# Mixture-of-experts stage: other row chunks, high parts by plain conversion, and the first expert's order of splitting

## The chip, the core and the metric

One core of one Trainium2 chip. The metric is the device time of one execution of the whole kernel in microseconds (us). The kernel before has a median of 5408.9 us in 3 runs (5398.77 to 5411.32). The engines: PE (TensorE, matrix products; its weight loads are listed as PEld and run beside the products), DVE (VectorE), ACT (ScalarE), POOL (GpSimd), and SP, which here only starts transfers.

## The reference, cut to what matters

Two transformer layers work on 16 batches of 512 tokens with 256 features. The change is in the last step only, a mixture of 8 experts in which each token goes to its best two experts:

```python
C = int(round(K * T * CAP_RATIO / E))          # K=2, T=8192, CAP_RATIO=1.05, E=8: 2150 slots an expert
buf = jnp.zeros((E, C + 1, D), xf.dtype).at[e_ord, pos].add(x_disp)[:, :C]
h = jax.nn.gelu(jnp.einsum('ecd,edh->ech', buf, W1) + b1[:, None, :], approximate=False)
y = jnp.einsum('ech,ehd->ecd', h, W2) + b2[:, None, :]
out = jnp.einsum('tk,tkd->td', cw, y_tk)       # cw: the gate's weights, y_tk: y of a token's two slots
```

D is 256 and the hidden width H is 1024. 2150 slots are 17 row tiles of 128 (`SLOT_TILES = 17`).

## The kernel before, in words

Eight stages run one after the other with a barrier between them (`STAGES`). The last, `experts` (L2384), takes the final 841 us of the trace. The earlier stages have filled a buffer in memory (`xbuf`) with each expert's rows. For expert n the 17 row tiles are worked in chunks of `QT = 4` tiles: `CHUNKS` (L2387) gives 4, 4, 4, 4 and 1 tiles, so `NC = 5`.

All products are made in float32r, a type that keeps fewer bits of a float32. To keep the accuracy each operand is split in a high and a low part, both float32r, and the product is high*high + high*low + low*high. The high part is got in two instructions: a mask (`bitwise_and` with `HIGH_BITS`) writes a cut copy, a conversion writes the cut copy as float32r. The low part is the operand minus the cut copy. This is done for the weights (`split_weights`, 8 pieces of 128x512 an expert: 0 to 3 are W1, 4 to 7 are W2), for the turned rows (`read_turned`, straight from PSUM) and for the hidden layer (`split_hidden`).

PE's order in an expert, for each chunk c: `hidden` for k = 0 to 7 (six matmuls each, L2653 to L2655; the moving operand has as many columns as the chunk has rows, 512 or 128), then `turn` of the *next* chunk (transposes, L2644, two for each tile), then `rows` for each tile i (16 matmuls, L2665 with 512 columns and L2667 with 256, into one of two PSUM banks). Before an expert PE waits for all 8 pieces of its weights, before a chunk's `hidden` for both `t_read` of its rows, in `rows` of tile 0 for each high and low part, and in `rows` of every tile for the bank of two tiles ago to be read (`y_read`).

ACT, for each k: the Gelu (L2562) of the PSUM bank, and after it the conversion of the cut copy of k-1 (`high_hidden`, L2552). The conversion of k = 7 follows at the chunk's end. Gelu k waits until the low part of k-4 is made.

DVE, in program order for each chunk: for k = 0 to 7 the mask (L2601) and the subtraction (L2604) of `split_hidden`; `read_turned` of the next chunk (two masks L2588, then L2592 and L2593 twice); then for each tile `read_rows` (L2611, L2613), and between tiles of chunks 1, 2 and 3 the pieces of the next expert's weights (`PIECES_IN`). Ahead of the first expert it splits all 8 pieces of weights and then reads the first turned rows.

POOL, for each tile: a multiplication by the gate's weight (L2523) and an indirect transfer that adds the rows to the output (L2527). SP loads rows and weights one or two chunks ahead. `expert_passes` (L2448) writes experts 0, 1, 6 and 7 straight out and runs experts 2 to 5 in a loop of two passes.

Of the kernel before, what the change touches and what calls it, by code (L numbers as in the profile page):

```python
# [8 lines left out]
ALU = mybir.AluOpType  # L9
AX = mybir.AxisListType.X  # L10
F32 = mybir.dt.float32
# [3 lines left out]
U32 = mybir.dt.uint32  # L15

P = 128
# [2366 lines left out]
def experts(nc, d):  # L2384


    CHUNKS = [(a, min(a + QT, SLOT_TILES)) for a in range(0, SLOT_TILES, QT)]  # L2387
    NC = len(CHUNKS)
    HC = HID // P
    NY = SLOT_TILES  # L2390
    RING = 4
# [4 lines left out]
    with ExitStack() as ctx:  # L2396
# [6 lines left out]
        w1_high = [s.sb(f"w1_high{i}", [P, KC, HID], F32R) for i in range(2)]  # L2403
        w1_low = [s.sb(f"w1_low{i}", [P, KC, HID], F32R) for i in range(2)]
        w2_both = [s.sb(f"w2_both{i}", [P, HC, 2, D], F32R) for i in range(2)]
        w_cut = [s.sb(f"w_cut{i}", [P, 512]) for i in range(2)]
        b1 = [s.sb(f"b1{i}", [P, HC]) for i in range(2)]
        b2 = [s.sb(f"b2{i}", [P, D]) for i in range(2)]
        x = [s.sb(f"x{i}", [P, QT, XROW]) for i in range(2)]
        to_token = [s.sb(f"to_token{i}", [P, QT], U32) for i in range(2)]  # L2410
        weight = [s.sb(f"weight{i}", [P, QT]) for i in range(2)]
        x_cut = [s.sb(f"x_cut{kc}", [P, SQ]) for kc in range(KC)]
        x_high = [s.sb(f"x_high{i}", [P, KC, SQ], F32R) for i in range(2)]
        x_low = [s.sb(f"x_low{i}", [P, KC, SQ], F32R) for i in range(2)]
        h = [s.sb(f"h{i}", [P, SQ]) for i in range(RING)]
        h_cut = [s.sb(f"h_cut{i}", [P, SQ]) for i in range(RING)]
        h_high = s.sb("h_high", [P, HC, SQ], F32R)
        h_low = s.sb("h_low", [P, HC, SQ], F32R)
        y_part = [s.sb(f"y_part{i}", [P, D]) for i in range(2)]
# [2 lines left out]
        const_in, w_in, x_in = s.sem("const_in"), s.sems("w_in", 2), s.sems("x_in", 2)  # L2422
        t_full, t_read, h_full, h_read, y_full, y_read = (
            s.sem(k) for k in ("t_full", "t_read", "h_full", "h_read", "y_full", "y_read"))
        x_cut_done, h_cut_done, h_high_done, h_low_done = (
            s.sem(k) for k in ("x_cut_done", "h_cut_done", "h_high_done", "h_low_done"))
        w_cut_done, w_high_done, w_low_done, y_part_done = (
            s.sem(k) for k in ("w_cut_done", "w_high_done", "w_low_done", "y_part_done"))
        y_out = s.sems("y_out", 2)
        tail_read, y_weighted = s.sem("tail_read"), s.sem("y_weighted")  # L2430
        carry, pool_carry = s.sem("carry"), s.sem("pool_carry")
# [26 lines left out]
        def following(n, par, c):  # L2458
            return (n, par, c + 1) if c + 1 < NC else (n + 1, 1 - par, 0)

        def piece(j):

            if j < 4:
# [2 lines left out]
            hc = slice(2 * (j - 4), 2 * (j - 4) + 2)  # L2466
            return (w2, (slice(None), hc, slice(None)), (w2_both, (slice(None), hc, 0, slice(None))),
                    (w2_both, (slice(None), hc, 1, slice(None))))

        def cut_of(j):  # L2470

            return w_cut[j % 2][:, :] if j < 4 else w_cut[j % 2][:, :].rearrange("p (c f) -> p c f", f=D)

        @block.sync
        def _(sp):
# [69 lines left out]
        @block.scalar  # L2545
        def _(act):
            act.sem_inc(h_read, 4)

            def high_hidden(n, c, k):
                cols = (CHUNKS[c][1] - CHUNKS[c][0]) * P  # L2550
                act.wait_ge(h_cut_done, (n * NC + c) * HC + k + 1)
                nc.scalar.copy(h_high[:, k, 0:cols], h_cut[k % RING][:, 0:cols]).then_inc(h_high_done, 1)  # L2552

            def one(n, par, last):
                act.wait_ge(w_in[par], 32 * (n - par) + 64)
                for c, (a, z) in enumerate(CHUNKS):
                    cols = (z - a) * P
                    for k in range(HC):
                        act.wait_ge(h_full, (n * NC + c) * HC + k + 1)
                        if not (isinstance(n, int) and n == 0 and c == 0 and k < RING):  # L2560
                            act.wait_ge(h_low_done, (n * NC + c) * HC + k + 1 - RING)
                        nc.scalar.activation(h[k % RING][:, 0:cols], hbank[k % 4][:, 0:cols], ACT.Gelu,  # L2562
                                             bias=b1[par][:, k:k + 1]).then_inc(h_read, 1)
                        if k > 0:
                            high_hidden(n, c, k - 1)
                    high_hidden(n, c, HC - 1)
            expert_passes(act, one)

        @block.vector
        def _(dve):  # L2570
            dve.sem_inc(y_read, 2 * NY)

            def split_weights(n, par, j):
                raw, part, (high, high_part), (low, low_part) = piece(j)
                if j == 0:
                    dve.wait_ge(w_in[par], 32 * (n - par) + 64)
                nc.vector.tensor_scalar(cut_of(j).bitcast(U32), raw[part].bitcast(U32), HIGH_BITS, None,  # L2577
                                        ALU.bitwise_and).then_inc(w_cut_done, 1)
                dve.wait_ge(w_cut_done, PIECES * n + j + 1)
                nc.vector.tensor_copy(high[par][high_part], cut_of(j)).then_inc(w_high_done, 1)  # L2580
                nc.vector.tensor_tensor(low[par][low_part], raw[part], cut_of(j), ALU.subtract).then_inc(w_low_done, 1)  # L2581

            def read_turned(n, par, c):
                cols = (CHUNKS[c][1] - CHUNKS[c][0]) * P
                pg = parity(par, c)
                for kc in range(KC):
                    dve.wait_ge(t_full, (n * NC + c) * 2 + kc + 1)
                    nc.vector.tensor_scalar(x_cut[kc][:, 0:cols].bitcast(U32), tbank[kc][:, 0:cols].bitcast(U32), HIGH_BITS, None,  # L2588
                                            ALU.bitwise_and).then_inc(x_cut_done, 1)
                for kc in range(KC):  # L2590
                    dve.wait_ge(x_cut_done, (n * NC + c) * 2 + kc + 1)
                    nc.vector.tensor_copy(x_high[pg][:, kc, 0:cols], x_cut[kc][:, 0:cols])  # L2592
                    nc.vector.tensor_tensor(x_low[pg][:, kc, 0:cols], tbank[kc][:, 0:cols], x_cut[kc][:, 0:cols],  # L2593
                                            ALU.subtract).then_inc(t_read, 1)

            def split_hidden(n, c, k):
                cols = (CHUNKS[c][1] - CHUNKS[c][0]) * P
                dve.wait_ge(h_read, (n * NC + c) * HC + k + 5)
                if not (isinstance(n, int) and n == 0 and c == 0 and k < RING):
                    dve.wait_ge(h_high_done, (n * NC + c) * HC + k + 1 - RING)  # L2600
                nc.vector.tensor_scalar(h_cut[k % RING][:, 0:cols].bitcast(U32), h[k % RING][:, 0:cols].bitcast(U32), HIGH_BITS,  # L2601
                                        None, ALU.bitwise_and).then_inc(h_cut_done, 1)
                dve.wait_ge(h_cut_done, (n * NC + c) * HC + k + 1)
                nc.vector.tensor_tensor(h_low[:, k, 0:cols], h[k % RING][:, 0:cols], h_cut[k % RING][:, 0:cols],  # L2604
                                        ALU.subtract).then_inc(h_low_done, 1)

            def read_rows(n, par, c, i):
                pg, number = parity(par, c), NY * n + CHUNKS[c][0] + i
                bank = (par + CHUNKS[c][0] + i) % 2
                dve.wait_ge(y_full, number + 1)  # L2610
                nc.vector.tensor_tensor(y_part[bank][:, :], ybank[bank][:, 1, :], b2[par][:, :], ALU.add).then_inc(y_part_done, 1)  # L2611
                dve.wait_ge(y_part_done, number + 1)
                nc.vector.tensor_tensor(y[pg][:, i, :], ybank[bank][:, 0, :], y_part[bank][:, :], ALU.add).then_inc(y_read, 1)  # L2613

            for j in range(PIECES):
                split_weights(0, 0, j)
            read_turned(0, 0, 0)

            def one(n, par, last):
                for c, (a, z) in enumerate(CHUNKS):  # L2620
                    for k in range(HC):
                        split_hidden(n, c, k)
                    if not (last and c == NC - 1):
                        read_turned(*following(n, par, c))
                    at_least(dve, y_out[parity(par, c)], scattered_before(n, par, c, parity(par, c)))
                    pieces = () if last else PIECES_IN.get(c, ())
                    for i in range(z - a):
                        read_rows(n, par, c, i)
                        for j in pieces[i * len(pieces) // (z - a):(i + 1) * len(pieces) // (z - a)]:
                            split_weights(n + 1, 1 - par, j)  # L2630
            expert_passes(dve, one)

        @block.tensor
        def _(pe):
# [36 lines left out]
            turn(0, 0, 0)  # L2671

            def one(n, par, last):
                pe.wait_ge(w_high_done, PIECES * n + PIECES)
                pe.wait_ge(w_low_done, PIECES * n + PIECES)
                for c, (a, z) in enumerate(CHUNKS):
                    pe.wait_ge(t_read, (n * NC + c) * 2 + 2)
                    for k in range(HC):
                        hidden(n, par, c, k)
                    if not (last and c == NC - 1):  # L2680
                        turn(*following(n, par, c))
                    for i in range(z - a):
                        rows(n, par, c, i)
            expert_passes(pe, one)
# [105 lines left out]
```

## Time and profile before

| | |
|---|---|
| median of 3 runs | 5408.9 us |
| the profiled execution | 5409.27 us, its span 5407.4 us |
| PE busy over the span | 4887.9 us (90%) |
| DVE, ACT, POOL busy | 3896.2 (72%), 2692.4 (50%), 1236.4 us (23%) |
| mean granted TensorE clock | 0.941 of full speed |

A busy PE is not PE at its peak: the end of a matmul is modelled and overlaps the next one, so what a matmul costs is read from start to start. In the rows below a timeline row gives the start in us from the span's start, the duration in us, engine, line, operation, out<-in with shapes and the count of merged instructions; in brackets the idle time of that engine just before, and what ended it.

### The profile page before, as it was taken

To read this page: it belongs to the slowest core of one execution; us is meant where nothing else is said; L and a number is where in the kernel's file an instruction comes from. 1 tells how busy PE (TensorE), PEld (TensorE's weight loads), DVE (VectorE), ACT (ScalarE), POOL (GpSimd) and SP (SyncE) were. 2 spreads that over 40 slices of the span, in tenths; PEclk is the share of its full clock that TensorE was granted. 3 is DMA by queue.
4 is the path that set the end of the run, shared out by engine and by line. 5 is a ranking of instruction groups with operands and counts; after the bars stand their busy time and mean duration, and the time that the engine had idled before them with its cause. 6 is when DMAs were issued, how large, how long until landed. Compare 5 with 4: busy or idle time off the path is not lost. (4 is left out here: it accounts for less than half of the span.)

```text
span 5407.4 us, 90976 instructions
## 1 busy us (share of the span) xinstructions
PE 4887.9 (90%) x28783; PEld 2800.2 (52%) x28784; DVE 3896.2 (72%) x7609; ACT 2692.4 (50%) x3563; POOL 1236.4 (23%) x964
## 2 busy tenths in 40 slices
PE   8979997997699999999999999999997911999999
PEld 4546665775244444443444444444432710888887
DVE  7766765664768888887888878888884831787786
ACT  2225552222337777776677767777764100444443
POOL 5620001222611010010010001000000345454454
PEclk9989998998889999999999999999998855999999
DMA  7765654223843323323323333323221654333332
GB/s 218 222 179 163 163 143 120 82 69 100 255 88 74 66 47 69 67 59 75 66 46 72 67 60 74 62 49 71 51 45 49 199 157 157 60 61 81 60 61 36
DMA packets 326812, 519.64 MB, mean 96 GB/s; under 512 B 50000, under 2 KB 242863, under 8 KB 324192
## 3 DMA queue, kind: packets, MB, share of 16 engines
q1 hardware_dynamic: 294816, 461.48, 35.0%
q0 software_dynamic: 28208, 51.82, 4.6%
q8 instruction: 226, 3.70, 0.3%
q14 instruction: 202, 1.65, 0.1%
q10 hardware_dynamic: 3360, 0.98, 0.1%
HBM read 254.97 MB, written 179.55 MB: 80 GB/s over the span
## 5 line engine op out<-in xcount | busy, mean ns | idle before, releaser
L1185 DVE TENSOR_REDUCE full_peak<-full_item 128x1 f32<-128x512 f32 (+2 forms) x3392 | 2035.3, 654 | 467.1 <-PE full_item L1252 461.6
L1155 ACT ACTIVATE full_prob<-full_score 128x1024 f32<-128x1024 f32 (+1 forms) x1792 | 1650.8, 961 | 641.4 <-PE full_score L1263 634.4
L1252 PE MATMUL full_item<-full_kst,full_qst 49*128 49x512 f32 (+1 forms) x4096 | 1204.1, 406 | 36.7 <-DVE full_peak L1185 24.3
L1263 PE MATMUL full_score<-full_qst,full_kst 51*128 51x512 f32 (+1 forms) x3328 | 1110.8, 448 | 21.2 <-ACT full_prob L1155 12.1
L1263 PEld LDWEIGHTS full_score<-full_qst,full_kst 51*128 51x128 f32 (+1 forms) x3328 | 480.5, 183 | 935.9 <-ACT full_prob L1155 602.3
L1277 PE MATMUL full_value<-full_prob,full_vaug 128*17 128x512 f32 x6656 | 886.5, 605 | 0.8 <-ACT full_raw L1142 0.7
L1252 PEld LDWEIGHTS full_item<-full_kst,full_qst 49*128 49x128 f32 x4096 | 630.7, 189 | 180.2 <-DVE full_peak L1185 129.8
L2562 ACT ACTIVATE moe_h<-moe_hbank,moe_b 128x512 f32<-128x512 f32 (+1 forms) x320 | 199.9, 625 | 453.8 <-PE moe_hbank L2655 447.8
L1100 POOL TENSOR_TENSOR full_low<-full_low,full_high 128x1601 f32<-128x1601 f32 x32 | 115.7, 3615 | 1194.3 <-DVE full_high L1171 1194.3
L2665 PE MATMUL moe_ybank<-moe_w_both,moe_h_high 128*128 128x512 f32 x1088 | 386.5, 399 | 0.0
L1096 POOL TENSOR_TENSOR full_low<-full_low,full_keep 128x1601 f32<-128x1601 f32 x32 | 116.0, 3624 | 1068.1 <-ACT full_low L1128 1068.1
L754 DVE TENSOR_REDUCE win_peak<-win_item 128x2 f32<-128x384 f32 x512 | 262.0, 552 | 124.0 <-PE win_item L794 117.1
L728 ACT ACTIVATE win_prob<-win_score 128x768 f32<-128x768 f32 x256 | 207.5, 811 | 266.5 <-PE win_score L808 263.3
L2667 PE MATMUL moe_ybank<-moe_w_both,moe_h_low 128*128 128x256 f32 x1088 | 304.6, 280 | 0.0
L2527 POOL DMA_INDIRECT out<-moe_y,moe_to_token x136 | 234.5, 1724 | 121.7 <-POOL moe_y L2523 86.9
L2653 PE MATMUL moe_hbank<-moe_x_high,moe_w_high 128*128 128x512 f32 (+1 forms) x640 | 236.6, 370 | 17.7 <-DVE moe_x_low L2593 15.7
L1277 PEld LDWEIGHTS full_value<-full_prob,full_vaug 128*17 128x17 f32 x6656 | 110.4, 95 | 246.9 <-issue 223.8
L2523 POOL TENSOR_SCALAR moe_y<-moe_y,moe_weight 128x256 f32<-128x256 f32 x136 | 194.6, 1431 | 190.8 <-issue 110.6
L2655 PE MATMUL moe_hbank<-moe_x_high,moe_w_low 128*128 128x512 f32 (+1 forms) x640 | 236.3, 369 | 0.0
L2654 PE MATMUL moe_hbank<-moe_x_low,moe_w_high 128*128 128x512 f32 (+1 forms) x640 | 235.9, 369 | 0.0
L2665 PEld LDWEIGHTS moe_ybank<-moe_w_both,moe_h_high 128*128 128x128 f32 x1088 | 204.2, 188 | 47.1
L1227 PE MATMUL full_score<-full_ctxT,full_wk 128*128 128x512 f32 (+1 forms) x512 | 218.5, 552 | 4.6 <-DMA full_ctxT<-in_ctxT 3.6
(274 smaller groups left out, 7197.3 us busy)
## 6 DMA issues: line engine op xcount, KB each, us to landing
full_kst<-full_high SPq DMA_DIRECT2D x256, 200.1 KB
full_ctxT<-in_ctxT SPq DMA_DIRECT2D x16, 1601.0 KB, 9.0
full_kst<-full_low SPq DMA_DIRECT2D x128, 200.1 KB
win_qst<-scratch_q SPq DMA_DIRECT2D x384, 64.0 KB, 2.7
full_qst<-scratch_q SPq DMA_DIRECT2D x384, 64.0 KB
scratch_xbuf<-ctxp_zero POOLq DMA_DIRECT2D x17, 1032.0 KB, 7.8
moe_x<-scratch_xbuf SPq DMA_DIRECT2D x32, 516.0 KB, 3.7
scratch_attn<-win_raw SPq DMA_DIRECT2D x64, 256.0 KB, 2.1
```

The lines of the kernel that those rows point to most:

```text
L754: nc.vector.tensor_reduce(peak[s.par][:, hq:hq + 2], src, AX, ALU.max).then_inc(item_read, 1)
L1155: nc.scalar.activation(prob[h][(s.par * PAIRS + t) % 2][0:rows, 0:banks, :], score[u % 2][0:rows, 0:banks, :], ACT.Exp, scale=SCALE).then_ ...
L1185: nc.vector.tensor_reduce(peak[s.par][:, hq:hq + len(qts), c], src, AX, ALU.max).then_inc(item_read, 1)
L1252: ins = nc.tensor.matmul(ps[:, at:at + z - a], qst[s.slot][rows, h // 2, qt * P:(qt + 1) * P].bitcast(F32R), kst[s.slot][rows, h // 2, a:z ...
L1263: ins = nc.tensor.matmul(score[u % 2][0:z - a, kt % 2, :], kst[s.slot][rows, h // 2, a:z].bitcast(F32R), qst[s.slot][rows, h // 2, :].bitc ...
L1277: ins = nc.tensor.matmul(value[32 * h:32 * h + VW, :], vaug[batch_par(s)][0:rows, kt, GROUP * s.slot + h, :], src, start=(kt == 0), stop=( ...
L2527: pool.indirect_dma_start(d["out"], bass.IndirectOffsetOnAxis(to_token[pg][:, i:i + 1], 0), y[pg][:, i, :], None, bounds_check=TOKENS + SL ...
L2653: nc.tensor.matmul(out, high, x_high[pg][:, kc, 0:cols], start=(kc == 0), stop=False)
L2654: nc.tensor.matmul(out, high, x_low[pg][:, kc, 0:cols], start=False, stop=False)
L2655: ins = nc.tensor.matmul(out, low, x_high[pg][:, kc, 0:cols], start=False, stop=(kc == KC - 1))
L2665: nc.tensor.matmul(bank[:, :, :], h_high[:, hc, i * P:(i + 1) * P], w2_both[par][:, hc, :, :], start=(hc == 0), stop=False, skip_group_che ...
L2667: ins = nc.tensor.matmul(bank[:, 0, :], h_low[:, hc, i * P:(i + 1) * P], w2_both[par][:, hc, 0, :], start=False, stop=(hc == HC - 1), skip ...
```

## The change

- `CHUNKS` is spread evenly over the same `NC = 5`. The formula gives the bounds 0, 4, 7, 11, 14, 17, so the chunks have 4, 3, 4, 3 and 3 tiles, in that order.
- The masks and the cut copies are gone. A high part is one conversion of the operand itself to float32r; the low part is the operand minus that high part, read back as float32. For the hidden layer the conversion stays on ACT and now comes first (after the Gelu of its k, as before behind the Gelu of k+1), and DVE's subtraction waits for it. For the turned rows the conversion reads PSUM.
- Ahead of the first expert DVE splits pieces 0 to 3 (W1), reads the first turned rows, and then splits pieces 4 to 7 (W2). PE waits for 4 pieces before an expert's first chunk, and for all 8 after the `hidden` and `turn` of chunk 0.

```diff
-    CHUNKS = [(a, min(a + QT, SLOT_TILES)) for a in range(0, SLOT_TILES, QT)]
-    NC = len(CHUNKS)
+    NC = -(-SLOT_TILES // QT)
+    CHUNKS = [(-(-c * SLOT_TILES // NC), -(-(c + 1) * SLOT_TILES // NC)) for c in range(NC)]
...
             def high_hidden(n, c, k):
                 cols = (CHUNKS[c][1] - CHUNKS[c][0]) * P
-                act.wait_ge(h_cut_done, (n * NC + c) * HC + k + 1)
-                nc.scalar.copy(h_high[:, k, 0:cols], h_cut[k % RING][:, 0:cols]).then_inc(h_high_done, 1)
+                act.wait_ge(h_read, (n * NC + c) * HC + k + 5)
+                nc.scalar.copy(h_high[:, k, 0:cols], h[k % RING][:, 0:cols]).then_inc(h_high_done, 1)
...
-                nc.vector.tensor_scalar(cut_of(j).bitcast(U32), raw[part].bitcast(U32), HIGH_BITS, None,
-                                        ALU.bitwise_and).then_inc(w_cut_done, 1)
-                dve.wait_ge(w_cut_done, PIECES * n + j + 1)
-                nc.vector.tensor_copy(high[par][high_part], cut_of(j)).then_inc(w_high_done, 1)
-                nc.vector.tensor_tensor(low[par][low_part], raw[part], cut_of(j), ALU.subtract).then_inc(w_low_done, 1)
+                nc.vector.tensor_copy(high[par][high_part], raw[part]).then_inc(w_high_done, 1)
+                dve.wait_ge(w_high_done, PIECES * n + j + 1)
+                nc.vector.tensor_tensor(low[par][low_part], raw[part], high[par][high_part].bitcast(F32),
+                                        ALU.subtract).then_inc(w_low_done, 1)
...
                 for kc in range(KC):
                     dve.wait_ge(t_full, (n * NC + c) * 2 + kc + 1)
-                    nc.vector.tensor_scalar(x_cut[kc][:, 0:cols].bitcast(U32), tbank[kc][:, 0:cols].bitcast(U32), HIGH_BITS, None,
-                                            ALU.bitwise_and).then_inc(x_cut_done, 1)
+                    nc.vector.tensor_copy(x_high[pg][:, kc, 0:cols], tbank[kc][:, 0:cols]).then_inc(x_high_done, 1)
                 for kc in range(KC):
-                    dve.wait_ge(x_cut_done, (n * NC + c) * 2 + kc + 1)
-                    nc.vector.tensor_copy(x_high[pg][:, kc, 0:cols], x_cut[kc][:, 0:cols])
-                    nc.vector.tensor_tensor(x_low[pg][:, kc, 0:cols], tbank[kc][:, 0:cols], x_cut[kc][:, 0:cols],
+                    dve.wait_ge(x_high_done, (n * NC + c) * 2 + kc + 1)
+                    nc.vector.tensor_tensor(x_low[pg][:, kc, 0:cols], tbank[kc][:, 0:cols], x_high[pg][:, kc, 0:cols].bitcast(F32),
                                             ALU.subtract).then_inc(t_read, 1)
...
-                nc.vector.tensor_scalar(h_cut[k % RING][:, 0:cols].bitcast(U32), h[k % RING][:, 0:cols].bitcast(U32), HIGH_BITS,
-                                        None, ALU.bitwise_and).then_inc(h_cut_done, 1)
-                dve.wait_ge(h_cut_done, (n * NC + c) * HC + k + 1)
-                nc.vector.tensor_tensor(h_low[:, k, 0:cols], h[k % RING][:, 0:cols], h_cut[k % RING][:, 0:cols],
+                dve.wait_ge(h_high_done, (n * NC + c) * HC + k + 1)
+                nc.vector.tensor_tensor(h_low[:, k, 0:cols], h[k % RING][:, 0:cols], h_high[:, k, 0:cols].bitcast(F32),
                                         ALU.subtract).then_inc(h_low_done, 1)
...
-            for j in range(PIECES):
+            for j in range(4):
                 split_weights(0, 0, j)
             read_turned(0, 0, 0)
+            for j in range(4, PIECES):
+                split_weights(0, 0, j)
...
-                pe.wait_ge(w_high_done, PIECES * n + PIECES)
-                pe.wait_ge(w_low_done, PIECES * n + PIECES)
+                pe.wait_ge(w_low_done, PIECES * n + 4)
...
+                    if c == 0:
+                        pe.wait_ge(w_low_done, PIECES * n + PIECES)
```

## Rows read from the trace of the kernel before

**Rows 1.** Experts' stage, busy us (instructions): PE PEld DVE ACT POOL; clock; DMA share; GB/s

```profile
4566.00:5407.00 841.00, 809.99 (x4368) 694.89 (x4368) 644.13 (x1344) 346.87 (x641) 399.08 (x352) 0.98 0.32 62
```

**Rows 2.** Timeline of PE, expert 6: the first instruction of some stretches

```profile
5219.40 0.40 PE L2653 MATMUL moe_hbank<-moe_x_high,moe_w_high 128*128 128x512 f32 x1
...
5230.35 1.03 PE L2644 MATMUL moe_tbank<-moe_ident,moe_x 128*128 128x128 f32 x8
5231.14 0.48 PE L2665 MATMUL moe_ybank<-moe_w_both,moe_h_high 128*128 128x512 f32 x1
...
5242.32 0.39 PE L2653 MATMUL moe_hbank<-moe_x_high,moe_w_high 128*128 128x512 f32 x1
...
5287.89 0.22 PE L2653 MATMUL moe_hbank<-moe_x_high,moe_w_high 128*128 128x128 f32 x1
...
5293.20 0.30 PE L2644 MATMUL moe_tbank<-moe_ident,moe_x 128*128 128x128 f32 x1
```

**Rows 3.** Timeline of PE where an expert ends and the next begins

```profile
4989.19 0.28 PE L2667 MATMUL moe_ybank<-moe_w_both,moe_h_low 128*128 128x256 f32 x1
4991.48 0.49 PE L2653 MATMUL moe_hbank<-moe_x_high,moe_w_high 128*128 128x512 f32 x1 [2.00 <-issue]
...
5296.80 0.28 PE L2667 MATMUL moe_ybank<-moe_w_both,moe_h_low 128*128 128x256 f32 x1
5297.95 0.47 PE L2653 MATMUL moe_hbank<-moe_x_high,moe_w_high 128*128 128x512 f32 x1 [0.88 <-DVE moe_x_low L2593]
```

**Rows 4.** PE's idle time ahead of `hidden`, all experts (releaser: us, times)

```profile
  DVE moe_x_low L2593: 15.7, 7
```

**Rows 5.** Timeline of DVE and PE, beginning of the experts' stage

```profile
4568.01 0.43 DVE L2577 TENSOR_SCALAR moe_w_cut<-moe_w 128x512 uint32<-128x512 uint32 x1 [54.03 <-DMA moe_b<-in_b]
4568.47 0.43 DVE L2580 CAST moe_w_high<-moe_w_cut 128x512 fp32r<-128x512 f32 x1
4568.81 0.68 DVE L2581 TENSOR_TENSOR moe_w_low<-moe_w,moe_w_cut 128x512 fp32r<-128x512 f32 x1
4569.42 0.42 DVE L2577 TENSOR_SCALAR moe_w_cut<-moe_w 128x512 uint32<-128x512 uint32 x1
...
4569.97 1.94 PE L2644 MATMUL moe_tbank<-moe_ident,moe_x 128*128 128x128 f32 x8 [198.13 <-DMA moe_x<-scratch_xbuf]
...
4579.20 1.28 DVE L2588 TENSOR_SCALAR moe_x_cut<-moe_tbank 128x512 uint32<-128x512 uint32 x2
4580.40 0.41 DVE L2592 CAST moe_x_high<-moe_x_cut 128x512 fp32r<-128x512 f32 x1
4580.73 0.68 DVE L2593 TENSOR_TENSOR moe_x_low<-moe_tbank,moe_x_cut 128x512 fp32r<-128x512 f32 x1
...
4582.60 0.77 PE L2653 MATMUL moe_hbank<-moe_x_high,moe_w_high 128*128 128x512 f32 x1 [10.69 <-DVE moe_x_low L2593]
```

**Rows 6.** Timeline of ACT and DVE at the end of a chunk's hidden layer

```profile
5230.55 0.69 ACT L2562 ACTIVATE moe_h<-moe_hbank,moe_b 128x512 f32<-128x512 f32 x1 [0.16 <-PE moe_hbank L2655]
5231.14 1.22 ACT L2552 CAST moe_h_high<-moe_h_cut 128x512 fp32r<-128x512 f32 x2
...
5231.73 0.69 DVE L2604 TENSOR_TENSOR moe_h_low<-moe_h,moe_h_cut 128x512 fp32r<-128x512 f32 x1
5232.34 1.28 DVE L2588 TENSOR_SCALAR moe_x_cut<-moe_tbank 128x512 uint32<-128x512 uint32 x2
...
5235.85 0.42 DVE L2613 TENSOR_TENSOR moe_y<-moe_ybank,moe_y_part 128x256 f32<-128x256 f32 x1
```

**Rows 7.** Timeline of POOL at the end of the kernel

```profile
5382.21 0.93 POOL L2523 TENSOR_SCALAR moe_y<-moe_y,moe_weight 128x256 f32<-128x256 f32 x1 [3.50 <-issue]
...
5385.12 1.48 POOL L2523 TENSOR_SCALAR moe_y<-moe_y,moe_weight 128x256 f32<-128x256 f32 x1
...
5388.56 1.47 POOL L2523 TENSOR_SCALAR moe_y<-moe_y,moe_weight 128x256 f32<-128x256 f32 x1
...
5398.88 0.92 POOL L2523 TENSOR_SCALAR moe_y<-moe_y,moe_weight 128x256 f32<-128x256 f32 x1 [2.83 <-issue]
```

More of the change, by code:

```diff
@@ L2405, in experts @@
         w2_both = [s.sb(f"w2_both{i}", [P, HC, 2, D], F32R) for i in range(2)]
-        w_cut = [s.sb(f"w_cut{i}", [P, 512]) for i in range(2)]
         b1 = [s.sb(f"b1{i}", [P, HC]) for i in range(2)]
@@ L2411, in experts @@
         weight = [s.sb(f"weight{i}", [P, QT]) for i in range(2)]
-        x_cut = [s.sb(f"x_cut{kc}", [P, SQ]) for kc in range(KC)]
         x_high = [s.sb(f"x_high{i}", [P, KC, SQ], F32R) for i in range(2)]
@@ L2415, in experts @@
         h = [s.sb(f"h{i}", [P, SQ]) for i in range(RING)]
-        h_cut = [s.sb(f"h_cut{i}", [P, SQ]) for i in range(RING)]
         h_high = s.sb("h_high", [P, HC, SQ], F32R)
@@ L2424, in experts @@
             s.sem(k) for k in ("t_full", "t_read", "h_full", "h_read", "y_full", "y_read"))
[L2425 to L2428, printed above, removed]
+        x_high_done, h_high_done, h_low_done = (s.sem(k) for k in ("x_high_done", "h_high_done", "h_low_done"))
+        w_high_done, w_low_done, y_part_done = (s.sem(k) for k in ("w_high_done", "w_low_done", "y_part_done"))
         y_out = s.sems("y_out", 2)
@@ L2468, in piece @@
                     (w2_both, (slice(None), hc, 1, slice(None))))
-        def cut_of(j):
-            return w_cut[j % 2][:, :] if j < 4 else w_cut[j % 2][:, :].rearrange("p (c f) -> p c f", f=D)
         @block.sync
@@ L2597, in split_hidden @@
                 cols = (CHUNKS[c][1] - CHUNKS[c][0]) * P
-                dve.wait_ge(h_read, (n * NC + c) * HC + k + 5)
-                if not (isinstance(n, int) and n == 0 and c == 0 and k < RING):
-                    dve.wait_ge(h_high_done, (n * NC + c) * HC + k + 1 - RING)
-                nc.vector.tensor_scalar(h_cut[k % RING][:, 0:cols].bitcast(U32), h[k % RING][:, 0:cols].bitcast(U32), HIGH_BITS,
-                                        None, ALU.bitwise_and).then_inc(h_cut_done, 1)
-                dve.wait_ge(h_cut_done, (n * NC + c) * HC + k + 1)
-                nc.vector.tensor_tensor(h_low[:, k, 0:cols], h[k % RING][:, 0:cols], h_cut[k % RING][:, 0:cols],
+                dve.wait_ge(h_high_done, (n * NC + c) * HC + k + 1)
+                nc.vector.tensor_tensor(h_low[:, k, 0:cols], h[k % RING][:, 0:cols], h_high[:, k, 0:cols].bitcast(F32),
                                         ALU.subtract).then_inc(h_low_done, 1)
```

## The prediction

> **What bounds the kernel now.** I read the busy time of the experts' stage first, then PE's timeline there, then the waits and the two ends of the stage. The stage takes 841 us, and PE has something in flight for 810 of them, DVE for 644, ACT for 347, POOL for 399 [rows 1]. The other stages aren't touched by the change, so only this one counts. PE's timeline shows one pattern eight times, about 101.5 us an expert. With 512 columns the 48 matmuls of a chunk's hidden layer take 10.95 us, 0.2281 us from start to start; the 64 matmuls of four row tiles (16 a tile, in pairs of one with 512 and one with 256 columns) take 11.18 us, 0.3494 us a pair; the 48 matmuls of the one-tile chunk take 5.31 us, 0.1106 us each [rows 2]. PE is idle in three places only. Before the first product it has waited 10.69 us for DVE's last low part of the turned rows [rows 5]. Between experts it waits for the same instruction: 15.7 us over seven waits, of which 10.69 is the first, so 5.0 us over six [rows 4]. And at one expert boundary it stands 2.00 us with "issue" as the cause, which is where the loop goes back to its start [rows 3]. After PE's last product comes a tail on DVE and POOL. So the kernel's end is set by how many microseconds PE's matmul stream takes, plus these gaps, and a cheaper DVE or ACT counts only where PE waits.
>
> **Part 1, the chunks (4, 4, 4, 4, 1 to 4, 3, 4, 3, 3).** The number of matmuls and the number of columns stay: 5 chunks of 48 for the hidden layer, 17 tiles of 16 for the rows, 34 transposes. What changes is that three chunks have 384 columns where two had 512 and one had 128. The trace has no matmul of 384 columns. Three widths are there: 512 at 0.2281, 256 at 0.3494 - 0.2281 = 0.1213, and 128 at 0.1106 us [rows 2]. At 2.4 GHz, the upper clock level (the stage's mean grant is 0.98 [rows 1]), the columns alone would be 0.2133, 0.1067 and 0.0533 us. So 512 and 256 columns both carry 0.0147 us on top, while 128 carries 0.057: that one is held by something that doesn't shrink with the columns. 384 lies between 256 and 512, so I take 0.1600 + 0.0147 = 0.1747 us, 8.39 us a chunk. An expert's hidden layer was 4 x 10.95 + 5.31 = 49.11 us and becomes 2 x 10.95 + 3 x 8.39 = 47.07: 2.04 us less, 16.3 us over 8 experts. Bounds: a straight line from 128 to 512 gives 0.1889 us for 384, 9.07 us a chunk and no gain at all; pure proportion to 512 gives 0.1711, 8.21 a chunk and 20.6 us. The 256 row lies far below the straight line (which would put it at 0.1498), so I stay near the middle value.
>
> What holds the 128 width is in the Trainium skill, "TensorE: Matmul & The Clock Gate", LDWEIGHTS: a weight load costs its 128 columns over 1.2 GHz, which by that page is 0.107 us; the trace's 0.1106 agrees. The same page, Back-to-back issue gap, puts a warm matmul at N/2.4 GHz plus 2.5 ns, 0.1625 us for 384 columns; for 512 it would give 0.2158 and the trace has 0.2281, so the trace decides.
>
> **Part 2, the wait between experts.** Now the last chunk has one row tile. PE's last product of it starts at 5296.80 and the next expert's first at 5297.95, 1.15 us later where 0.12 is normal [rows 3]. DVE must read the next 512 turned rows while PE has only 16 matmuls, 2.8 us. After the change the last chunk has three tiles and 8.4 us of row matmuls to cover the same reading, which itself gets shorter. The idle time is 5.0 us in six waits [rows 4], and each also costs some 0.15 us beyond it (1.15 - 0.12 - 0.88), so 5.9 us go. The seventh boundary (2.00, issue) is the loop's jump; the wait for DVE lies beneath it. I take nothing off there; at most its 2.0 us could go.
>
> **Part 3, the beginning.** A piece of weights takes DVE 0.46 for the mask, 0.34 for the conversion, 0.61 for the subtraction, from start to start, 1.41 us together [rows 5]. Without the mask, 1.07. PE's first product waits for the eight pieces and the turned rows. Now it will wait for four: 4 x 1.07 = 4.3, from 4568.0 to 4572.3; the transposes are through at 4571.9 [rows 5]. Then the turned rows: two operations from PSUM took 1.20 us (4579.20 to 4580.40), and from there to PE's start were 2.20 us, with two conversions of 0.33 (4580.40 to 4580.73) in it that go. New: 1.20 + 2.20 - 0.66 = 2.74 us, so PE starts at 4575.0 rather than 4582.6: 7.6 us. Bounds for the conversion out of PSUM, which the trace doesn't show: 0.33 each as out of SBUF (0.5 us more gain), 0.60 each as the mask had, or 1.2 each if such a conversion were twice that (1.2 us less gain). The mask, also one operand in and one out, is the nearest row. The four W2 pieces moved behind (4.3 us of DVE) end at about 4579.3. The first hidden product takes PE six matmuls and ACT's first Gelu follows, so DVE's first subtraction is wanted after 4579; the W2 pieces are wanted some 12 us later, at the first row products. SP's load of the next weights waits for all eight pieces; it started after them at 4579.2 and starts at about the same time. So these hide.
>
> The rule on this conversion speaks against part of the change: the Trainium skill, "VectorE: DVE Perf Modes", Why PSUM operands drop a tier, says that a float32 operand from PSUM runs at the plain rate while a one-source float32 operation within SBUF can run at twice it. The rows agree (0.60 against 0.33). So of each pair mask and conversion of turned rows the cheap one goes.
>
> **Part 4, the masks elsewhere.** DVE sheds a mask of some 0.4 us (the weights' mask has 0.43 [rows 5]) in each of 8 x 40 hidden pieces and the rest of the masks, perhaps 150 us of work, all of it beside PE. I price it at nothing; its cover is the matmul stream, and DVE had time left. But the hidden layer's chain gets longer, as high and low parts are now made one after the other. At the end of a 4-tile chunk [rows 6]: Gelu 7 starts at 5230.55, the two conversions 6 and 7 run to 5232.36, and the low part, which began at 5231.73, can begin only at 5232.4 and ends at 5233.1, 0.7 later than before. PE wants it in the eighth pair of the first row tile: 5231.14 + 7 x 0.349 + 0.23 = 5233.8 [rows 2]. 0.7 us are left. Queued behind it on DVE are the next turned rows and the first reading of row products, for which the third tile's matmuls wait. That reading ended at 5236.27 [rows 6]; it starts 0.7 later and saves 2 x 0.33, so 5236.3, and the third tile begins at 5231.14 + 2 x 2.80 = 5236.7. 0.4 us are left. For 384 columns all of these are shorter. ACT needs 0.59 + 0.61 = 1.20 us for each k at 512 columns against PE's 1.37; at 384 some 0.95 against 1.05 (by its fixed share, estimated from the same rows). Cost nothing, but with thin cover. If it is gone, each of the 39 chunk ends costs what it is late.
>
> **Part 5, the tail.** The last chunk has three tiles instead of one, so POOL has a queue. From multiplication to multiplication it needs 2.91 and then 3.44 us [rows 7], 6.35 for two, against PE's 5.6; and a multiplication behind a transfer takes 1.48 instead of 0.92. The end moves 0.7 + 0.6 = 1.3 us back.
>
> **Sum**: -16.3 - 5.9 - 7.6 + 1.3 = -28.5 us. The profiled execution took 5409.3, its span 5407.4 and 1.9 around it; that is 0.4 above the median of 5408.9. From the one 5380.8, from the other 5380.4. I predict 5380.5.
>
> **Rivals.** (A) The width brings nothing: 384 columns cost 0.189 us because the weight load or something between loads and products counts in. For it: 128 columns clearly sit on such a floor. Against: 256 columns don't. Then -28.5 + 16.3 = -12.2, 5397. (B) 384 columns are nearly free of the extra 0.0147 us, by the page's formula above as a mechanism of this kernel: products of this width wait for nothing between them. With 0.1625 us, 7.80 a chunk, an expert gains 49.11 - 21.90 - 23.40 = 3.8, and the whole is -30.5 - 12.2 = -42.7, 5366. Against: both wider rows carry the 0.0147. (C) The loop's jump gets cheaper too, since PE isn't late there any more: up to 2.0 more, and with the proportional width -34.8, 5374. (D) The other side: the longer chain at a chunk's end starves PE at the third row tile. It decides from 0.4 us of lateness. Every 0.1 us beyond costs 3.9 us over 39 ends; it turns slower than before beyond 0.7 + 0.4 = 1.1 us, as when each of the two conversions out of PSUM took 1.2 us instead of 0.6 and each subtraction read its float32r operand 0.2 slower. At 1.6 us late it would be -28.5 + 47 = +18, 5427. Against: the rows have 0.60 us an instruction out of PSUM and 0.7 for such a subtraction [rows 5, 6]. (E) The change doesn't do what it says: if the conversion kept all the bits, the low parts would be zero; that would alter the result's accuracy and no time.
>
> **Numbers.** Forecast 0.76, A 0.09, B 0.05, C 0.07, D 0.03. The runs before spread over 12 us, so I count 0.3% (16 us) as what can be told from no change. Faster by more: forecast, B and C, 0.88. Within: A, 0.09. Slower: D, 0.03. The range goes from 5371 (C and some spread of the runs) to 5394 (half of the width's gain missing and spread).
>
> **What would show it.** Right: hidden chunks of 384 columns take 8.4 us from first to last; PE's first product at about 4575; no idle time for `moe_x_low` between experts but the jump's 2 us; no idle time of PE within chunks; POOL's last transfer about 8 us after PE's end. Wrong: 9 us for the 384 chunks (A); PE idle before the third tile of a chunk, released by DVE's row reading, or inside the first tile by a low part (D).

## The result and the profile after

The changed kernel takes 5369.2 us (median of 4 runs, 5360.9 to 5372.0) against 5407.6 for the kernel before on the same chip: a ratio of 0.993, 95% interval 0.9914 to 0.9945, some 38 us less. A later comparison (`after_again` below) gave 0.9922 (0.9909 to 0.9936). Forecast were 28.5 us less, 5380.5 us, and a range of 5371 to 5394 us: the direction was right, the time lies 1.8 us below the range.

The profiled execution took 5369.95 us, its span is 5368.2, 39.2 shorter than before. The experts' stage in the view of [rows 1], 804 us now, DVE busy 460 instead of 644:

```profile
4564.00:5368.00 804.00, 785.92 (x4368) 705.46 (x4368) 459.95 (x880) 342.96 (x641) 378.79 (x352) 0.99 0.34 65
```

PE's timeline in expert 6, as [rows 2 and 3]: from the last row product of expert 5 on, then each stretch's first instruction.

```profile
5161.89 0.28 PE L2652 MATMUL moe_ybank<-moe_w_both,moe_h_low 128*128 128x256 f32 x1
5162.00 0.39 PE L2638 MATMUL moe_hbank<-moe_x_high,moe_w_high 128*128 128x512 f32 x1
...
5172.91 0.82 PE L2629 MATMUL moe_tbank<-moe_ident,moe_x 128*128 128x128 f32 x6
5173.49 0.47 PE L2650 MATMUL moe_ybank<-moe_w_both,moe_h_high 128*128 128x512 f32 x1
...
5184.66 0.34 PE L2638 MATMUL moe_hbank<-moe_x_high,moe_w_high 128*128 128x384 f32 x1
...
5193.00 1.04 PE L2629 MATMUL moe_tbank<-moe_ident,moe_x 128*128 128x128 f32 x8
```

A chunk of 512 columns takes 10.91 us (5162.00 to 5172.91), one of 384 takes 8.34 (5184.66 to 5193.00; 8.33 is the median of 24), which is 0.1735 us a matmul. Between experts 5 and 6 PE goes on after 0.11 us; before, the six boundaries without the loop's jump had 1.0 to 1.2 us from start to start (1.15 in the one of [rows 3]). The loop's boundary is the only idle time left in PE's stream:

```profile
4965.15 0.28 PE L2652 MATMUL moe_ybank<-moe_w_both,moe_h_low 128*128 128x256 f32 x1
4966.27 0.50 PE L2638 MATMUL moe_hbank<-moe_x_high,moe_w_high 128*128 128x512 f32 x1 [0.84 <-issue]
```

The beginning, as [rows 5]: DVE begins at 4565.42, PE's first product comes 6.84 us later (14.59 before).

```profile
4565.42 0.43 DVE L2568 CAST moe_w_high<-moe_w 128x512 fp32r<-128x512 f32 x1 [53.59 <-DMA moe_b<-in_b]
4565.88 0.69 DVE L2570 TENSOR_TENSOR moe_w_low<-moe_w,moe_w_high 128x512 fp32r<-128x512 f32 x1
4566.49 0.42 DVE L2568 CAST moe_w_high<-moe_w 128x512 fp32r<-128x512 f32 x1
...
4569.68 1.28 DVE L2578 CAST moe_x_high<-moe_tbank 128x512 fp32r<-128x512 f32 x2
4570.88 1.28 DVE L2581 TENSOR_TENSOR moe_x_low<-moe_tbank,moe_x_high 128x512 fp32r<-128x512 f32 x2
...
4572.26 0.76 PE L2638 MATMUL moe_hbank<-moe_x_high,moe_w_high 128*128 128x512 f32 x1 [3.28 <-issue]
```

A conversion out of PSUM costs 0.60 us from start to start, as the mask did. At the end of a chunk's hidden layer, as [rows 6], ACT, then DVE:

```profile
5173.11 0.69 ACT L2553 ACTIVATE moe_h<-moe_hbank,moe_b 128x512 f32<-128x512 f32 x1 [0.17 <-PE moe_hbank L2640]
5173.70 1.13 ACT L2543 CAST moe_h_high<-moe_h 128x512 fp32r<-128x512 f32 x2
```

```profile
5174.34 1.29 DVE L2587 TENSOR_TENSOR moe_h_low<-moe_h,moe_h_high 128x512 fp32r<-128x512 f32 x2 [0.67 <-ACT moe_h_high L2543]
5175.55 1.02 DVE L2578 CAST moe_x_high<-moe_tbank 128x384 fp32r<-128x384 f32 x2
...
5177.86 0.42 DVE L2596 TENSOR_TENSOR moe_y<-moe_ybank,moe_y_part 128x256 f32<-128x256 f32 x1
```

The first row reading ends at 5178.28. The third row tile's products begin 2 x 2.795 us after 5173.49, at 5179.08: 0.8 us of cover. With 384 columns and 512 to be read next it is 0.97 (5198.42 against 5193.79 + 5.6, from the same views), and in chunk 3, with 384 columns and 384 to be read next, 1.4. And POOL at the end, as [rows 7]: three multiplications, 2.87 and 3.45 us apart; the tail after PE's last product is 11.3 us, 9.9 before.

```profile
5352.61 0.92 POOL L2514 TENSOR_SCALAR moe_y<-moe_y,moe_weight 128x256 f32<-128x256 f32 x1 [6.14 <-issue]
...
5355.48 1.49 POOL L2514 TENSOR_SCALAR moe_y<-moe_y,moe_weight 128x256 f32<-128x256 f32 x1
...
5358.93 1.47 POOL L2514 TENSOR_SCALAR moe_y<-moe_y,moe_weight 128x256 f32<-128x256 f32 x1
```

**Where the time went**, summed over all stretches of PE's stream by their first instructions, in us:

| | before | after | difference | forecast |
|---|---|---|---|---|
| DVE's first instruction to PE's first product | 14.59 | 6.84 | -7.75 | -7.6 |
| hidden layers, at the full clock (40 chunks) | 392.8 | 374.5 | -18.3 | -16.3 |
| hidden layers, extra while the clock is low | 3.6 | 1.6 | -2.0 | 0 |
| idle between experts, six | 6.0 | 0 | -6.0 | -5.9 |
| idle at the loop's boundary | 2.2 | 1.0 | -1.2 | 0 |
| row products themselves | 384.7 | 382.0 | -2.7 | 0 |
| transposes | 25.7 | 25.6 | -0.1 | 0 |
| tail after PE's last product | 9.9 | 11.3 | +1.4 | +1.3 |
| DVE's first instruction to the end | 839.4 | 802.8 | -36.6 | -28.5 |
| all that lies ahead of it | 4568.0 | 4565.4 | -2.6 | 0 |

### The profile page after: what moved, and what is told of

Same layout as the page of the kernel before. It is cut to its first block and busy times, and to the rows that moved or that the text cites. A ratio compares the mean times of both kernels' runs of the same rounds, so it can differ in the third digit from the quotient of the medians.

```text
span 5368.2 us, 90200 instructions
## 1 busy us (share of the span) xinstructions
PE 4868.7 (91%) x28783; PEld 2813.1 (52%) x28784; DVE 3710.4 (69%) x7145; ACT 2687.3 (50%) x3563; POOL 1212.4 (23%) x964
## 5 line engine op out<-in xcount | busy, mean ns | idle before, releaser
L2553 ACT ACTIVATE moe_h<-moe_hbank,moe_b 128x384 f32<-128x384 f32 (+1 forms) x320 | 199.8, 625 | 431.8 <-PE moe_hbank L2640 395.5
L2587 DVE TENSOR_TENSOR moe_h_low<-moe_h,moe_h_high 128x384 fp32r<-128x384 f32 (+1 forms) x320 | 194.2, 617 | 209.8 <-ACT moe_h_high L2543 205.3
L2638 PE MATMUL moe_hbank<-moe_x_high,moe_w_high 128*128 128x384 f32 (+1 forms) x640 | 229.1, 358 | 4.1 <-issue 4.1
L2640 PE MATMUL moe_hbank<-moe_x_high,moe_w_low 128*128 128x384 f32 (+1 forms) x640 | 228.6, 357 | 0.0
L2639 PE MATMUL moe_hbank<-moe_x_low,moe_w_high 128*128 128x384 f32 (+1 forms) x640 | 228.3, 357 | 0.0
L2514 POOL TENSOR_SCALAR moe_y<-moe_y,moe_weight 128x256 f32<-128x256 f32 x136 | 183.1, 1346 | 182.3 <-issue 103.2
```

Source lines behind the costliest of these rows:

```text
L2638: nc.tensor.matmul(out, high, x_high[pg][:, kc, 0:cols], start=(kc == 0), stop=False)
L2639: nc.tensor.matmul(out, high, x_low[pg][:, kc, 0:cols], start=False, stop=False)
L2640: ins = nc.tensor.matmul(out, low, x_high[pg][:, kc, 0:cols], start=False, stop=(kc == KC - 1))
```

## The experiments

All ratios are to the kernel before, timed beside each. "Stage" is the time from DVE's first instruction of the experts' stage to the end of the span (839.4 and 802.8 us above).

**One part at a time.** `chunks_only` is the kernel before with one edit:

```diff
-    CHUNKS = [(a, min(a + QT, SLOT_TILES)) for a in range(0, SLOT_TILES, QT)]
-    NC = len(CHUNKS)
+    NC = -(-SLOT_TILES // QT)
+    CHUNKS = [(-(-c * SLOT_TILES // NC), -(-(c + 1) * SLOT_TILES // NC)) for c in range(NC)]
```

> The kernel before with chunks of 4, 3, 4, 3 and 3 tiles alone; masks and order of the beginning as before. My theory: nearly all that was missing from the forecast belongs to the chunks: hidden layers -20 us over PE's stretches, idle time between experts -6, row matmuls at the quicker of their two paces -2.7, the loop's boundary -2.8 (1.1 us of idle instead of 2.3, and the clock stays up), tail +1.3: 27 to 30 us less in all. Rival: the quicker rows and the cheaper boundary come from DVE's smaller load (no masks), then some 22 us less, the boundary still with 2.3 us and a slow clock behind it, and four-tile row stretches of both 11.18 and 11.38 us.

Measured: ratio 0.9949 (0.9935 to 0.9962), some 28 us; stage 811.2, 28.2 less. Hidden layers 376.7 (396.4 before), every four-tile row stretch but the first 11.18 us, the boundary with 1.0 us and the clock up. So these belong to the chunks, with the masks still on DVE.

`masks_only` is the changed kernel with the old `CHUNKS` and the old beginning: plain conversions alone.

> The kernel before with the plain conversions alone; chunks 4, 4, 4, 4, 1 and the old order of the beginning. My theory: beginning 8 x 0.34 + 0.66 = 3.4 us shorter, waits between experts from 1.0 to some 0.5 us each (-3), nothing within chunks: 5 to 8 us less. The loop's boundary tells two ideas apart: if the jump begins when PE's last wait before it ends and takes a fixed time, the 2.3 us stay; if it adds 1.2 us to the wait for the turned rows, it falls to 1.7. Rival of the longer chain (D): slower than before.

Ratio 0.9988 (0.9979 to 0.9997), stage 832.6, 6.8 less, as expected, so the longer chain doesn't make it slower on the whole. But "nothing within chunks" isn't quite what the trace shows. In the fourth chunk of an expert only two transposes stand between the hidden layer and the row products; there the eighth low part ends at 5177.32, and PE's eighth pair starts 0.29 us after the product before it instead of 0.11 to 0.12:

```profile
5177.18 0.28 PE L2650 MATMUL moe_ybank<-moe_w_both,moe_h_low 128*128 128x256 f32 x1
5177.47 0.47 PE L2648 MATMUL moe_ybank<-moe_w_both,moe_h_high 128*128 128x512 f32 x1
```

That makes the row stretch 11.47 us instead of 11.38, some 0.9 us over eight experts: the second form of (D), a low part that comes too late, at a small price. The boundary:

```profile
4989.84 0.28 PE L2650 MATMUL moe_ybank<-moe_w_both,moe_h_low 128*128 128x256 f32 x1
4992.16 0.49 PE L2636 MATMUL moe_hbank<-moe_x_high,moe_w_high 128*128 128x512 f32 x1 [2.04 <-issue]
```

The turned rows were ready at 4989.97 (DVE's subtraction there), and PE still stands until 4992.16. So the 2.3 us aren't the wait for the rows plus something: they lie beside it. The other six boundaries fell from 1.1 to some 0.3 us from start to start, where 0.12 is normal: 0.2 us of waiting each is left of 1.0, less than the 0.5 expected.

`head_only` is the kernel before with the new beginning:

```diff
-            for j in range(PIECES):
+            for j in range(4):
                 split_weights(0, 0, j)
             read_turned(0, 0, 0)
+            for j in range(4, PIECES):
+                split_weights(0, 0, j)
...
-                pe.wait_ge(w_high_done, PIECES * n + PIECES)
-                pe.wait_ge(w_low_done, PIECES * n + PIECES)
+                pe.wait_ge(w_low_done, PIECES * n + 4)
...
+                    if c == 0:
+                        pe.wait_ge(w_low_done, PIECES * n + PIECES)
```

> The kernel before with the new order of the beginning alone. My theory: PE's first product 4 x 1.41 = 5.6 us sooner after DVE's first instruction, and nothing else: 5.6 us less in all. Rival: what is gained is given back at the first row products, which wait for the second weight: 0 to 2 us less.

PE's first product comes 8.86 us after DVE's first instruction (5.7 less), nothing is given back; stage 832.9, 6.5 less; ratio 0.9984 (0.9975 to 0.9993). The 0.8 us more are the first chunk's clock (12.4 us instead of 12.8) and boundaries 0.4 us shorter in all.

The three gains add up to 41.5 us, the change has 36.6: the waits between experts are shortened by masks and chunks alike, and the beginning too is counted twice in part.

`before_again` is the kernel before, unchanged.

> The kernel before, unchanged, profiled again. It tells how far two profiles of one program differ: if the experts' stage again starts at 4558.5 us within 0.5 us, the 2.1 us by which it started sooner in the changed kernel belong to the change; if it wanders by 2 us, they don't. Its four-tile row stretches should again be of 11.18 and 11.38 us in the same order if the pace is set by the program, in another order if by chance. Timed: ratio 1.000.

Ratio 1.0002 (0.9993 to 1.0011), stage 839.8 against 839.4; its four-tile row stretches have 11.18 and 11.38 us in the same order but for the first. The stage begins with SP's load of the identity; here the start of that in this profile and in that of `head_only`, whose seven earlier stages are the same code:

```profile
4558.78 0.34 SPq L2476 DMA_DIRECT2D moe_ident<-in_ident  x1
```

```profile
4566.44 0.35 SPq L2476 DMA_DIRECT2D moe_ident<-in_ident  x1
```

Over the 14 profiles of this study it lies between 4549.5 and 4566.4, though two profiles of one program agree within 0.8 us (before 4558.5 and 4558.8, changed 4556.4 and 4555.6). So the 2.6 us ahead of the stage can't be laid to any step of the change; whether they come with the program or by chance is open.

**The width.** `c44432` is the changed kernel with chunks of 4, 4, 4, 3, 2 tiles:

```diff
-    CHUNKS = [(-(-c * SLOT_TILES // NC), -(-(c + 1) * SLOT_TILES // NC)) for c in range(NC)]
+    CHUNKS = [(0, 4), (4, 8), (8, 12), (12, 15), (15, 17)]
```

> The changed kernel with chunks of 4, 4, 4, 3 and 2 tiles, so that an expert has one chunk of 256 columns. Theory of a fixed extra per matmul (columns at 2.4 GHz plus 14 to 15 ns, down to 256 columns): a 256-column chunk takes 48 x 0.121 = 5.8 us, an expert's hidden layer 46.9 us against 46.8, the whole within 3 us of the changed kernel. Rival, a cost that grows smoothly below 512 (a straight line from 128): the 256 chunk takes 7.2 us, 11 us more over the kernel. The loop's boundary: if the jump takes 4.4 us from PE's last wait, its idle time falls to 0.5 us or less, since that wait is over before the last two tiles' products.

A 256-column chunk of its profile, first product to the transposes: 5246.83 to 5252.59.

```profile
5246.83 0.28 PE L2638 MATMUL moe_hbank<-moe_x_high,moe_w_high 128*128 128x256 f32 x1
5246.95 0.28 PE L2639 MATMUL moe_hbank<-moe_x_low,moe_w_high 128*128 128x256 f32 x1
5247.07 0.28 PE L2640 MATMUL moe_hbank<-moe_x_high,moe_w_low 128*128 128x256 f32 x1
```

5.76 us a chunk (all eight 5.75 or 5.76), 0.1200 each: a fixed 13 to 14 ns on top of the columns from 256 to 512 (0.1200, 0.1735, 0.2274), and a floor of 0.11 at 128. The straight line is refuted, and so is the 2.5 ns of the rival (B). Ratio 0.9935 (0.9922 to 0.9947), stage 805.1. The boundary had 1.2 us of idle time, not 0.5 or less: that part of the expectation missed (below).

`c44333` has the same chunk sizes in another order, by the edit `CHUNKS = [(0, 4), (4, 8), (8, 11), (11, 14), (14, 17)]`.

> The changed kernel with the same chunk sizes in the order 4, 4, 3, 3, 3. Same columns, same matmuls: the same time within 2 us, but the quick and slow rhythm of the row products may fall on other stretches, worth 0.2 us each and up to 3 us in all. Rival: the order matters (weight pieces meet other chunks, two four-tile chunks in a row starve at the third row tile), then over 5 us slower than the changed kernel.

Ratio 0.9937 (0.9925 to 0.9949), stage 805.6, 2.8 more than the changed kernel. Row products take 1.9 us more, as 16 three-tile stretches instead of 9 run at 8.55 us and 5 four-tile ones at 11.38; the rest is the clock at the very start (13.4 us for the first chunk instead of 12.5, a value that differs from program to program, 12.4 to 13.7). No starving, though the first chunk's cover, with 512 columns behind 512, is only 0.5 to 0.6 us.

**The cover of the longer chain.** `dve_late1` and `dve_late3` put one or three copies of 1024 columns on DVE ahead of each chunk's row reading. The copies' results aren't used.

```diff
+        spare = [s.sb(f"spare{i}", [P, 1024], F32R) for i in range(3)]
...
                     at_least(dve, y_out[parity(par, c)], scattered_before(n, par, c, parity(par, c)))
+                    for r in range(3):
+                        nc.vector.tensor_copy(spare[r][:, :], w1_high[par][:, 0, :])
```

> The changed kernel with one extra copy of 1024 columns on DVE, some 0.6 us, ahead of each chunk's first row reading. In the changed kernel's trace that reading ends 0.8 to 1.0 us before the third row tile's products start. Theory: the cover of the longer chain is 0.8 us, so nothing is lost (0 to 3 us in all). Rival, my forecast's 0.4 us of cover: 0.2 us lost in each of 39 chunks, 8 us.

Ratio 0.9935 (0.9922 to 0.9948), PE's stream 786.0 us against 784.7, and of that 1.2 is the first chunk's clock. 0.6 us late costs nothing.

> The changed kernel with three such copies, some 1.8 us, ahead of each chunk's first row reading. Theory: 0.8 to 1.0 us late in each of 39 chunks, 30 to 40 us more than the changed kernel, about as slow as the kernel before; PE idle ahead of the third tile's first product. If PE had other cover, the time would stay.

Ratio 1.0006 (0.9997 to 1.0014), stage 843.6, 40.8 more. PE stands in 39 chunks, as here, released by DVE's row reading:

```profile
5197.27 0.28 PE L2655 MATMUL moe_ybank<-moe_w_both,moe_h_low 128*128 128x256 f32 x1
5198.26 0.50 PE L2653 MATMUL moe_ybank<-moe_w_both,moe_h_high 128*128 128x512 f32 x1 [0.70 <-DVE moe_y L2597]
```

The three copies take 1.8 us from start to start, the cover was 0.8 to 1.1 us at 31 chunk ends and 1.4 at the eight with 384 columns behind 384. By the forecast's price that is some 31 us; the row stretches grew by 38.7 (a four-tile one from 11.18 to 12.41). So (D) is a real mechanism, about a quarter dearer than the forecast's 3.9 us for each 0.1, and in the changed kernel it begins at 0.8 to 1.4 us, not at 0.4.

**The loop's boundary.** `before_pe_straight` writes PE's experts out; the other engines keep their loop.

```diff
-            expert_passes(pe, one)
+            for n in range(EXPERTS):
+                one(n, n % 2, n == EXPERTS - 1)
```

> The kernel before with PE's eight experts written straight out, without the loop (the other engines keep theirs). In four profiles with a one-tile last chunk PE stood 2.3 to 2.5 us at the loop's boundary and the clock was low for the next 12 matmuls or so; PE's first product came 4.4 to 4.6 us after the end of the last low part that PE had waited for. Theory: the jump costs that, so straight code leaves the usual 1.0 us of waiting for the turned rows and the clock stays up: -1.2 and -1.7, 2.9 us less in PE's stream. Rival: the boundary is set by another engine's jump or a transfer, then 2.3 us stay.

The boundary between experts 3 and 4, which was [rows 3]'s 2.29 us from start to start:

```profile
4989.55 0.28 PE L2667 MATMUL moe_ybank<-moe_w_both,moe_h_low 128*128 128x256 f32 x1
4990.80 0.48 PE L2653 MATMUL moe_hbank<-moe_x_high,moe_w_high 128*128 128x512 f32 x1 [0.97 <-DVE moe_x_low L2593]
```

1.25 us as at any other expert, and the hidden chunk after it takes 11.03 us; with the loop it took 12.64. The granted clock (third number from the end, as a share of 2.4 GHz) in the view of [rows 1], first with the loop, 1.2 GHz for 3.4 us, then without it, 2.4 GHz throughout:

```profile
4992.70:4996.10 3.40, 3.40 (x9) 2.62 (x8) 0.57 (x2) 0.69 (x1) 1.61 (x1) 0.51 1.05 378
```

```profile
4990.80:4996.10 5.30, 5.30 (x23) 4.39 (x24) 1.02 (x4) 1.47 (x3) 2.53 (x2) 1.00 0.82 268
```

So PE's own jump is the cause, and it takes the clock with it. The profile also has the transfers of instructions (packets, MB, share of the DMA engines). From 4980 to 4996 us, with the loop:

```profile
q8 instruction: 3, 0.05, 1.2%
q14 instruction: 2, 0.02, 0.2%
```

The same stretch without it:

```profile
q14 instruction: 2, 0.02, 0.2%
```

Only PE's code was changed, so q8 is PE's queue. It moves 16384 bytes about every 23 us elsewhere in the stage, but three times within 8 us at the loop's jump. In all eleven profiles with the loop PE's next product starts 2.7 to 3.1 us after the second of these transfers starts. PE's stream, first product to last, is 813.5 us against 814.9 and 815.4; it would be near 812.6 had the first chunk not had 13.7 us this time. Ratio 0.9991 (0.9982 to 1.0), so the timing alone doesn't show the gain.

`after_pe_straight` is the same edit on the changed kernel.

> The changed kernel with PE's experts written straight out. Theory: the remaining 1.0 us of idle time at the boundary goes and nothing else, 1.0 us less in PE's stream, which timing can't tell from nothing.

No idle time is left in PE's stream; 784.9 us against 784.7, as the first chunk took 1.1 us more and hid it. Ratio 0.9924 (0.991 to 0.9937).

`both_more` is `after_pe_straight` with an earlier start: two pieces of W1 ahead of the turned rows.

```diff
         def piece(j):
+            j = (0, 2, 1, 3, 4, 5, 6, 7)[j]
...
-            for j in range(4):
+            for j in range(2):
...
-                pe.wait_ge(w_low_done, PIECES * n + 4)
+                pe.wait_ge(w_low_done, PIECES * n + 2)
...
+                        if c == 0 and k == 4:
+                            pe.wait_ge(w_low_done, PIECES * n + 4)
```

> A version meant to beat both: the changed kernel with PE's experts straight out, and with the pieces of W1 in the order 0, 2, 1, 3, so that ahead of the first expert DVE splits two pieces (the first 512 hidden features), reads the turned rows, and splits the rest; PE waits for two pieces, and for four ahead of k = 4. Theory: PE's first product 1.2 us sooner (DVE then waits for the transposes at 3.6 us after its start, so not the full 2.1), and the boundary's 1.0 us: some 2 us less than the changed kernel, about 0.9925 of the kernel before. Rival: PE stalls at k = 4 for the later pieces, then nothing is won.

PE's first product 5.61 us after DVE's first instruction (6.84), stage 801.0 against 802.8 and 802.9. Ratio 0.9918 (0.9905 to 0.9932), the lowest of all, median 5366.2 beside 5368.1 for the changed kernel on the same chip. The trace shows the gain of 1.9 us; the timing can't tell it from nothing.

`after_again` is the changed kernel, unchanged.

> The changed kernel unchanged, profiled and timed again beside the others: 0.993 of the kernel before within 0.0015; PE's stream from its first product to its last within 1 us of 784.5 us; the start of the experts' stage anywhere between 4556 and 4567 us, as earlier profiles of programs with identical earlier stages had it.

0.9922 (0.9909 to 0.9936), stream 784.8, stage 802.9, stage's start 4555.6.

## Why the prediction was right in kind and too small

**The chunks (Part 1).** Right, and it carries the most. The middle value of 0.1747 us was 0.1735, and 512 columns take 10.91 rather than 10.95 us: the forecast took its 10.95 from a chunk that follows a slow row stretch [rows 2]. Eight experts of 0.24 us each are the 2.0 us between -16.3 and -18.3. Rival (A), no gain from the width, is refuted by 24 chunks of 8.33 us and by the 256 columns of `c44432`, rival (B) by the same rows.

**The row products (no term of the sum: put at nothing without a reason).** 2.7 us. The forecast took 2.8 us a tile before and after. In fact a row stretch runs in one of two steady rhythms, 11.18 or 11.38 us for four tiles (0.3494 or 0.3556 a pair on average), and keeps it to its end. The forecast's stretch from 5231.14 is a quick one; the one before it, up to the 5219.40 of [rows 2], is slow:

```profile
5208.02 0.48 PE L2665 MATMUL moe_ybank<-moe_w_both,moe_h_high 128*128 128x512 f32 x1
```

Before, 19 of the 32 four-tile stretches had the slow one; afterwards none, and of the three-tile stretches the eight of chunk 3 and one other (8.55 instead of 8.40). The order repeats from profile to profile and goes with the chunks, not with the masks (`chunks_only` has the new order, `masks_only` the old). What starts the slow rhythm isn't settled.

**The waits between experts (Part 2).** The six went, 6.0 us. The seventh was the step that failed: "I take nothing off there". It lost 1.2 us of idle time, and 1.6 us of low clock behind it. `masks_only` and `before_pe_straight` show the mechanism. PE's jump back takes some 4.4 us from the last wait ahead of it. With one row tile after the last hidden chunk, that wait (for the eighth low part) ends late: PE's next product came 4.4 to 4.6 us after it in four profiles. With three tiles the last wait is for the first tile's bank to be read, ahead of the third tile. PE's next product came 4.3 to 5.0 us after the end of that reading in six profiles, but 3.0 to 3.8 us of products were still to be done then, and only 0.8 to 1.4 us showed (1.0 in the changed kernel). Not the last wait alone decides: in `c44432` it was over 5.9 us ahead and 1.2 us showed. There the second instruction transfer began 3.1 us after the wait, in the other ten profiles 1.3 to 1.8 us, so the sequencer came to the jump later; that it can run only so far ahead is likely, but wasn't tried apart. After 2.2 to 2.4 us of standing the granted clock went from 2.4 to 1.2 GHz (weight loads of 0.33 instead of 0.19 us); after 0.8 to 1.4 us it stayed up in every profile. The Trainium skill, "Runtime: NRT & Kernel Launch", Instruction fetch mechanics, has the rule: a taken branch outside the fetched pages must wait for a transfer of its target. The transfers on q8 and the straight code agree. A rival (C) of the forecast named the place, with a chance of 0.07.

**The beginning (Part 3).** Right within 0.15 us, the 0.60 us out of PSUM too; `head_only` gives back nothing.

**The longer chain (Part 4).** Priced at nothing, rightly. Its cover is 0.8 us and more, not 0.4: the forecast worked out the 4-tile chunk before a 4-tile chunk, which the new order never has; each four-tile chunk is followed by 384 columns, quicker to read. For the case that it worked out, `c44333` and `c44432` have 0.5 to 0.6 us. Rival (E), of the accuracy, would change no time and wasn't tried.

**The tail (Part 5).** 1.4 us for 1.3.

So of the 38 us some 28.5 were forecast by steps that held. Missing were 2.8 us (boundary and clock) and 2.7 (rhythm), both put at nothing, and 2.0 (widths, mis-sized): small each, all of one sign. Another 2.6 us lie ahead of the stage, and no step explains them. The range allowed 9.5 us below the forecast, which was just short. That the time fell below it by 1.8 us is partly chance: without the 2.6 us ahead of the stage it would have been inside, and the forecast started from 5408.9 us where the kernel before had 5407.6 beside the changed one.

## What to carry to other kernels

A product with 128 columns took 0.11 us, one with 256 took 0.12: spread the tiles so that no chunk falls below 256 columns, and the small last chunk also stops being the place where nothing covers the next expert's reading and the loop's jump. When an engine is busy nearly all of a stage, look for all of its idle time by start-to-start distances, and ask of each how long its cause began earlier; a jump's cost is hidden by work queued ahead of it. Move the other engines' work freely, but measure its cover: 0.6 us more was free here, 1.8 us more cost the whole gain.

## What the runs showed of the hardware that wasn't expected

- Float32r products with float32r weights run at the columns over 2.4 GHz plus 13 to 14 ns from 256 to 512 columns (0.1200, 0.1735, 0.2274 us), and at 0.11 us for 128.
- The same pairs of products run at 0.3494 or 0.3556 us on average through a whole stretch, in the same order in two profiles of one program but for the first stretch.
- A jump back on PE costs 4.3 to 5.0 us from PE's last wait ahead of it (5.9 in `c44432`), of which 0.8 to 2.4 showed; three 16384-byte instruction transfers go with it, and PE's next product starts 2.7 to 3.1 us after the second.
- Code that is the same reaches the same point between 4549.5 and 4566.4 us in different programs, but within 0.8 us in two profiles of one (two programs were profiled twice).
